# 192 unused bytes per partition in front of the first MLP layer's split input

## The chip, the core and the metric

The kernel runs on one core of one Trainium2 chip. The metric is the device time of one execution in microseconds (us); the times shown are of repeated executions of the same kernel.

## What is computed

A transformer block with modulated layer norms, for 8 batches of 1024 rows of 256 features, all in 32-bit floats. Per batch (cut to what matters):

```python
h = layernorm(x) * (1 + ca) + sa
attn = softmax((h * w_lhs) @ (h * w_rhs).T) @ h        # 1024 x 1024 scores
x = x + ga * attn
h = layernorm(x) * (1 + cb) + sb
x = x + gb * (relu(h @ W1 + b1) @ W2 + b2)             # 256 -> 1024 -> 256
```

The factors `sa`, `ca`, `ga`, `sb`, `cb`, `gb` are made once from a small input. The change touches the first product of the last line, `h @ W1`, and nothing else.

## The kernel before

**Split operands.** To keep precision, each 32-bit operand of a large product is held as two rounded parts, hi and lo (type fp32r), and a product is the sum of three matmuls: hi by hi, hi by lo, lo by hi. So the first layer has `W1hi`, `W1lo` as stationary operand (the weights that TensorE loads, 128 columns of 4 bytes, 512 bytes in each partition, per matmul) and `h2hi`, `h2lo` as moving operand (512 columns, 2048 bytes in each partition). `h2hi` is written by ScalarE (L819) and `h2lo` by VectorE (L1153), from the turned layer norm in `featT`.

**Steps.** The work of a batch is cut into steps, and the order of the steps on every engine is written out by hand (L29 to L170): in the loop over batches 2 to 6 (L121, `STEPS`), TensorE's list mixes the attention of this batch with the MLP of the batch before. On TensorE `SC.n` is a tile of scores (L649 to L651, operands `Lhi`, `Llo`, `Rhi`, `Rlo`), `AV.n` a tile of the attention product (L762, L763, L766, moving operand `V`, stationary `Phi`, `Plo`), `F.n` a group of the first MLP layer (L660 to L662) and `G.n` one of the second (L582, L583, L588, moving operand `W2hi`, `W2lo`, stationary `hid_hi`, `hid_lo`). Before `F.n` TensorE waits until ScalarE has read the result bank (`col_read`), and at the first of a half for `h2lo`.

One first-layer group is six matmuls, each with its own load of weights:

```python
for kk in range(DK):                                                          # DK = 2
    nc.tensor.matmul(col[n % 2][:], W1hi[:, kk, tile], h2hi[:, kk, cols], ...)   # L660
    nc.tensor.matmul(col[n % 2][:], W1hi[:, kk, tile], h2lo[:, kk, cols], ...)   # L661
    last = nc.tensor.matmul(col[n % 2][:], W1lo[:, kk, tile], h2hi[:, kk, cols], ...)   # L662
```

There are 16 groups a batch and 8 batches: 128 groups, 768 matmuls, 256 of each line. A second-layer group takes 12 matmuls of 256 columns, an attention tile 8 pairs (L762 with 258 columns, L763 with 256) and then 8 of L766 (258 columns).

**Where the operands lie.** Tensors are placed in each partition one behind the other, in the order in which L259 to L320 name them. With the sizes of that list the first bytes of those that matter are, and what is left of them when whole multiples of 512 are taken off:

| tensor | first byte | mod 512 |
|---|---|---|
| W1hi, W1lo | 17024, 25216 | 128 |
| W2hi, W2lo | 33408, 41600 | 128 |
| Phi, Plo | 87104, 99392 | 64 |
| Lhi, Llo, Rhi, Rlo | 111680 and on, 8192 apart | 64 |
| V | 144448, rows of 2080 bytes, second half 1040 behind | 64, and 32 more each row |
| hid_hi, hid_lo | 198336, 204480 | 192 |
| h2hi, h2lo | 210624, 218816 | 192 |

A tile of `W1` moves by 512 bytes, a half of `h2` by 2048 and `kk` by 4096, so all slices of one tensor have the same place mod 512. In what follows the **offset** is the place of the matmul's moving operand less the place of the weights that are loaded during it, those of the next matmul, mod 512. Within first-layer groups it is 192 - 128 = 64. In second-layer groups it is 128 - 192 = 448, in scores 0; in L766 it goes up by 32 from matmul to matmul: 16, 48, 80, 112, 144, 176, 208, and 240 for the eighth when `Phi`'s weights follow.

Other tensors lie behind `h2lo`: row statistics, maxima and other small ones (L310 to L320), up to byte 228,064.

Of the kernel before, what the change touches and what calls it, by code (L numbers as in the profile page):

```python
# [11 lines left out]
P = 128  # L12
# [200 lines left out]
def block_kernel(nc, x, w_lhs, w_rhs, W1, b1, W2, b2, cT, wmod, out):  # L213
# [39 lines left out]
    with ExitStack() as ctx:  # L253
        sb = lambda name, shape, dt=F32: ctx.enter_context(nc.sbuf_tensor(name, shape, dt))
# [51 lines left out]
        featT = sb("featT", [P, DK, HR])  # L306
        hid = sb("hid", [P, 2, HR])
        hid_hi, hid_lo = sb("hid_hi", [P, RING, HR], F32R), sb("hid_lo", [P, RING, HR], F32R)
        h2hi, h2lo = sb("h2hi", [P, DK, ROWS], F32R), sb("h2lo", [P, DK, ROWS], F32R)
        stats, stats1 = sb("stats", [P, HT, 6]), sb("stats1", [P, HT, 6])  # L310
        mv1, nm1, rs1 = sb("mv1", [P, T, 2]), sb("nm1", [P, T]), sb("rs1", [P, T])
# [1017 lines left out]
```

## Time and profile before

| | |
|---|---|
| median of 3 runs | 678.64 us (678.5 to 679.3) |
| the profiled execution's own time | 679.18 us |
| its span, first to last instruction | 677.4 us, 13532 instructions |
| TensorE busy, matmuls / weight loads | 672.5 us (99%) / 620.4 us (92%) |
| VectorE, ScalarE, GpSimd busy | 545.9 (81%), 500.2 (74%), 295.2 us (44%) |
| granted TensorE clock | 1.00 of full |

How to read it: a matmul's duration in the rows runs from its first column to its modelled end, and neighbours overlap. What a matmul costs in a stream is the distance from its start to the next one's start, called its spacing below; the timeline gives starts to 0.01 us, so spacings are taken over several matmuls. In the timeline, neighbours of one line are merged into one row (x8), which has the start of the first; a later window shows the row from a later one on.

### The profile page before, as it was taken

The numbers are of one execution on the slowest core, as the hardware profiler recorded it, in microseconds if no ns is written. First come the engines' busy times: TensorE is split into PE (matmuls) and PEld (weight loads), VectorE is DVE, ScalarE is ACT, GpSimd is POOL, SyncE is SP. The second block draws the span as 40 slices with busy tenths as digits, with TensorE's granted clock in tenths as the row PEclk, the third lists the DMA queues.
The fourth block names the chain that finished last, engine by engine and source line by source line (L and its number), as shares of the span: only waits on it lengthen the run. The fifth ranks groups of instructions, "written<-read, shape, count | busy, mean of one in ns | idle before, by whom it ended". The sixth has DMA issues, their size and how long they took to land.

```text
span 677.4 us, 13532 instructions
## 1 busy us (share of the span) xinstructions
PE 672.5 (99%) x4551; PEld 620.4 (92%) x4551; DVE 545.9 (81%) x1139; ACT 500.2 (74%) x749; POOL 295.2 (44%) x311
## 2 busy tenths in 40 slices
PE   9999999999999999999999999999999999999998
PEld 8688889998999999999999989999899999999897
DVE  4798889887899879998799887988789987778321
ACT  2376787976889777895878949888688976747563
POOL 3551365225353345442645235542535334615544
PEclk9999999999999999999999999999999999999999
DMA  8131664237632377124671256513763246311210
GB/s 295 55 81 62 194 188 148 72 97 237 194 96 74 123 238 231 48 89 149 202 210 62 93 186 195 145 62 124 216 195 84 75 146 197 97 41 65 85 48 31
DMA packets 72897, 88.57 MB, mean 131 GB/s; under 512 B 6880, under 2 KB 64800, under 8 KB 72864
## 3 DMA queue, kind: packets, MB, share of 16 engines
q1 hardware_dynamic: 72864, 88.15, 41.6%
q8 instruction: 18, 0.29, 0.2%
q14 instruction: 15, 0.12, 0.1%
HBM read 51.66 MB, written 36.47 MB: 130 GB/s over the span
## 4 chain that ended last, share of the span: by engine, by line
PE 99%; DVE 0%; DMA 0%; issue 0%; SPq 0%
PE col L662 9%; PE col L661 9%; PE col L660 9%; PE acc L582 8%; PE acc L583 8%; PE acc L588 8%; PE score L766 8%; PE score L762 8%; PE score L763 8%; PE score L650 4%; PE score L651 4%; PE score L649 4%; PE score L755 4%; PE score L623 2%; PE score L551 1%; PE score L727 1%
## 5 line engine op out<-in xcount | busy, mean ns | idle before, releaser
L1249 POOL TENSOR_TENSOR hid_lo<-hid,hid_hi 128x512 fp32r<-128x512 f32 x127 | 175.9, 1387 | 258.3 <-ACT hid_hi L791 257.6
L787 ACT ACTIVATE hid<-col,b1T 128x512 f32<-128x512 f32 x128 | 87.1, 681 | 72.6 <-PE col L662 67.8
L582 PE MATMUL acc<-W2hi,hid_hi 128*128 128x256 f32 x480 | 118.0, 280 | 0.0
L583 PE MATMUL acc<-W2lo,hid_hi 128*128 128x256 f32 x480 | 116.6, 277 | 0.0
L762 PE MATMUL score<-V,Phi 128*128 128x258 f32 x448 | 108.7, 281 | 0.0
L763 PE MATMUL score<-V,Phi 128*128 128x256 f32 x448 | 108.5, 281 | 0.0
L662 PE MATMUL col<-h2hi,W1lo 128*128 128x512 f32 x256 | 101.0, 395 | 0.0
L660 PE MATMUL col<-h2hi,W1hi 128*128 128x512 f32 x256 | 100.7, 393 | 0.0
L661 PE MATMUL col<-h2lo,W1hi 128*128 128x512 f32 x256 | 100.7, 393 | 0.0
L791 ACT ACTIVATE hid_hi<-hid 128x512 fp32r<-128x512 f32 x128 | 81.0, 633 | 23.2 <-PE acc L588 15.6
L582 PEld LDWEIGHTS acc<-W2hi,hid_hi 128*128 128x128 f32 x480 | 90.3, 188 | 1.4
L583 PEld LDWEIGHTS acc<-W2lo,hid_hi 128*128 128x128 f32 x480 | 90.2, 188 | 1.5
L762 PEld LDWEIGHTS score<-V,Phi 128*128 128x128 f32 x448 | 85.0, 190 | 0.7
L763 PEld LDWEIGHTS score<-V,Phi 128*128 128x128 f32 x448 | 84.1, 188 | 0.7
L588 PE MATMUL acc<-W2hi,hid_lo 128*128 128x256 f32 x480 | 76.4, 276 | 0.0
L876 ACT ACTIVATE soft<-soft 128x1024 f32<-128x1024 f32 x56 | 58.3, 1051 | 22.4 <-DVE soft L1027 11.8
L1064 DVE TENSOR_TENSOR Plo<-soft,Phi 128x1024 fp32r<-128x1024 f32 x56 | 70.9, 1283 | 2.1 <-ACT Phi L892 2.1
L588 PEld LDWEIGHTS acc<-W2hi,hid_lo 128*128 128x128 f32 x480 | 64.4, 188 | 0.0
L766 PE MATMUL score<-V,Plo 128*128 128x258 f32 x448 | 62.8, 282 | 0.0
L892 ACT ACTIVATE Phi<-soft 128x1024 fp32r<-128x1024 f32 x56 | 58.9, 1052 | 0.6
L1236 POOL TENSOR_SCALAR nm<-mv 128x4 f32<-128x4 f32 x32 | 11.6, 362 | 108.6 <-DVE mv L1085 64.9
L662 PEld LDWEIGHTS col<-h2hi,W1lo 128*128 128x128 f32 x256 | 48.2, 188 | 10.6
(168 smaller groups left out, 1476.5 us busy)
## 6 DMA issues: line engine op xcount, KB each, us to landing
block_rows<-blocks SPq DMA_DIRECT2D x29, 512.0 KB, 2.8
blocks<-block_rows SPq DMA_DIRECT2D x116, 128.0 KB, 2.9
x_cur<-x SPq DMA_DIRECT2D x16, 512.0 KB, 3.9
ln_t<-x SPq DMA_DIRECT2D x14, 512.0 KB, 4.8
score_blocks<-stage SPq DMA_DIRECT2D x14, 512.0 KB, 2.9
S<-score_blocks SPq DMA_DIRECT2D x56, 128.0 KB, 3.0
S<-quarter_blocks SPq DMA_DIRECT2D x56, 96.0 KB, 2.6
out<-x_mlp SPq DMA_DIRECT2D x8, 512.0 KB, 5.3
```

What stands on the lines that cost most here:

```text
L582: nc.tensor.matmul(o, hi, W2hi[:, it, :], start=(it == 0 and (apart or t % 2 == 0)), stop=False, skip_group_check=True)
L583: nc.tensor.matmul(o, hi, W2lo[:, it, :], start=False, stop=False, skip_group_check=True)
L588: last = nc.tensor.matmul(o, lo, W2hi[:, it, :], start=False, stop=(it == FT - 1), skip_group_check=True)
L660: nc.tensor.matmul(col[n % 2][:], W1hi[:, kk, tile], h2hi[:, kk, cols], start=(kk == 0), stop=False)
L661: nc.tensor.matmul(col[n % 2][:], W1hi[:, kk, tile], h2lo[:, kk, cols], start=False, stop=False)
L662: last = nc.tensor.matmul(col[n % 2][:], W1lo[:, kk, tile], h2hi[:, kk, cols], start=False, stop=(kk == DK - 1))
L762: nc.tensor.matmul(o, Phi[:, slot, t, :], V[:, t, 0:VW], start=(t == 0), stop=False)
L763: nc.tensor.matmul(o[:, 0:D], Phi[:, slot, t, :], V[:, t, VP:VP + D], start=False, stop=False)
L766: last = nc.tensor.matmul(o, Plo[:, slot, t, :], V[:, t, VP:VP + VW], start=False, stop=(t == T - 1))
L787: nc.scalar.activation(hid[:, n % 2, :], col[n % 2][:], ACT.Relu, bias=b1T[:, n % FT:n % FT + 1]).then_inc(col_read, 1)
L791: nc.scalar.activation(hid_hi[:, n % RING, :], hid[:, n % 2, :], ACT.Copy).then_inc(hid_hi_done, 1)
L1249: G.tensor_tensor(hid_lo[:, n % RING, :], hid[:, n % 2, :], hid_hi[:, n % RING, :].bitcast(F32), ALU.subtract).then_inc(hid_lo_done, 1)
```

## The change

A tensor of 48 floats, 192 bytes in each partition, is placed between `hid_lo` and `h2hi`. Nothing reads or writes it. All that lies behind it, `h2hi`, `h2lo` and the small tensors, moves up by 192 bytes.

```diff
         hid_hi, hid_lo = sb("hid_hi", [P, RING, HR], F32R), sb("hid_lo", [P, RING, HR], F32R)
+        sb("before_h2", [P, 48])
         h2hi, h2lo = sb("h2hi", [P, DK, ROWS], F32R), sb("h2lo", [P, DK, ROWS], F32R)
         stats, stats1 = sb("stats", [P, HT, 6]), sb("stats1", [P, HT, 6])
```

`h2hi` then begins at byte 210,816, which is 384 mod 512, and the offset within first-layer groups is 384 - 128 = 256.

## Rows read from the trace of the kernel before

**Rows 1.** The page: busy time by engine, and the granted clock in 40 slices.

```profile
span 677.4 us, 13532 instructions
...
PE 672.5 (99%) x4551; PEld 620.4 (92%) x4551; DVE 545.9 (81%) x1139; ACT 500.2 (74%) x749; POOL 295.2 (44%) x311
...
PEclk9999999999999999999999999999999999999999
```

**Rows 2.** The chain that ended last: shares of the 677.4 us span by line.

```profile
by line: PE col L662 8.8%; PE col L661 8.7%; PE col L660 8.7%; PE acc L582 8.2%; PE acc L583 8.1%; PE acc L588 8.0%; PE score L766 7.9%; PE score L762 7.8%; PE score L763 7.8%; PE score L650 4.4%; PE score L651 4.3%; PE score L649 4.3%; PE 
```

**Rows 3.** Groups by line (busy us, mean ns of one | idle before).

```profile
L662 PE MATMUL col<-h2hi,W1lo 128*128 128x512 f32 x256 | 101.0, 395 | 0.0
L660 PE MATMUL col<-h2hi,W1hi 128*128 128x512 f32 x256 | 100.7, 393 | 0.0
```

**Rows 4.** TensorE's timeline (start us, us, what), first-layer stretch behind the second layer.

```profile
182.44 0.39 PE L660 MATMUL col<-h2hi,W1hi 128*128 128x512 f32 x1
182.66 0.39 PE L661 MATMUL col<-h2lo,W1hi 128*128 128x512 f32 x1
182.89 0.39 PE L662 MATMUL col<-h2hi,W1lo 128*128 128x512 f32 x1
183.13 0.39 PE L660 MATMUL col<-h2hi,W1hi 128*128 128x512 f32 x1
...
185.19 0.28 PE L762 MATMUL score<-V,Phi 128*128 128x258 f32 x1
```

**Rows 5.** The same timeline, first-layer stretch behind the attention product.

```profile
188.04 0.40 PE L660 MATMUL col<-h2hi,W1hi 128*128 128x512 f32 x1
...
188.75 0.40 PE L660 MATMUL col<-h2hi,W1hi 128*128 128x512 f32 x1
...
192.24 0.28 PE L582 MATMUL acc<-W2hi,hid_hi 128*128 128x256 f32 x1
...
192.72 0.28 PE L582 MATMUL acc<-W2hi,hid_hi 128*128 128x256 f32 x1
```

**Rows 6.** Windows (busy us of each engine, PEclk the granted clock) over both stretches.

```profile
182.44:185.19 2.75, 2.75 (x14) 2.26 (x13) 2.72 (x4) 1.15 (x2) 0.00 (x0) 1.00 0.81 230
188.04:192.24 4.20, 4.20 (x20) 3.41 (x19) 4.08 (x8) 3.62 (x5) 2.51 (x3) 1.00 1.03 264
```

**Rows 7.** Timeline of TensorE, a settled second-layer group, 256 columns each.

```profile
172.43 0.28 PE L582 MATMUL acc<-W2hi,hid_hi 128*128 128x256 f32 x1
...
173.79 0.39 PE L660 MATMUL col<-h2hi,W1hi 128*128 128x512 f32 x1
```

**Rows 8.** Timeline of TensorE, score matmuls of 256 columns, no offset between operands.

```profile
155.17 0.28 PE L650 MATMUL score<-Rlo,Lhi 128*128 128x256 f32 x1
...
155.77 0.40 PE L649 MATMUL score<-Rhi,Lhi 128*128 128x512 f32 x1
```

**Rows 9.** Timeline of TensorE, one run of eight L766, read from its start and later ones.

```profile
626.04 1.12 PE L766 MATMUL score<-V,Plo 128*128 128x258 f32 x8
...
626.52 0.53 PE L766 MATMUL score<-V,Plo 128*128 128x258 f32 x3
...
626.65 0.40 PE L766 MATMUL score<-V,Plo 128*128 128x258 f32 x2
...
626.89 0.28 PE L766 MATMUL score<-V,Plo 128*128 128x258 f32 x1
627.00 0.28 PE L762 MATMUL score<-V,Phi 128*128 128x258 f32 x1
```

**Rows 10.** Groups by line: who writes the split input, and who follows a first-layer group.

```profile
L787 ACT ACTIVATE hid<-col,b1T 128x512 f32<-128x512 f32 x128 | 87.1, 681 | 72.6 <-PE col L662 67.8 <-POOL hid_lo L1249 4.3
...
L1153 DVE TENSOR_TENSOR h2lo<-featT,h2hi 128x512 fp32r<-128x512 f32 x32 | 21.6, 712 | 10.6 <-ACT h2hi L819 10.6
...
L819 ACT ACTIVATE h2hi<-featT 128x512 fp32r<-128x512 f32 x32 | 20.2, 633 | 1.0
```

## The prediction

> **What bounds the kernel.** The page is read first: TensorE is busy for 672.5 of 677.4 us, VectorE for 81%, and the granted clock is full, the 2.4 GHz level, in all 40 slices [rows 1]. The chain that ended last is TensorE nearly throughout; the three first-layer lines hold 8.8 + 8.7 + 8.7 = 26.2% of it [rows 2], 177.5 us of the span. Over 768 matmuls that is 231.1 ns each. They had no idle time before them [rows 3]. So no wait can be taken away here, and what the change can alter is how fast one matmul follows the next.
>
> The timeline shows that this is not one number. In a stretch behind the second layer, 12 first-layer matmuls take from 182.44 to 185.19, 2.75 us, 229 ns each [rows 4]. In a stretch behind the attention product, 18 of the same matmuls take from 188.04 to 192.24, 4.20 us, 233.3 ns each [rows 5]. Same line, shape, clock and addresses mod 512, and the matmuls busy throughout [rows 6]. In the first the starts 182.44, .66, .89 and 183.13 show steps of 0.22, 0.23, 0.24: the delay isn't even over the three lines.
>
> What would it be with no delay? The nearest row is a settled second-layer group: 12 matmuls of 256 columns from 172.43 to 173.79, 113.3 ns each, with weight loads back to back as well [rows 7]. Twice that for 512 columns is 226.7 ns, my estimate of the floor. Against it score matmuls of the same 256 columns with offset 0 take five in 0.60 us (155.17 to 155.77), 120.0 ns each, 6.7 over the floor [rows 8]; and the first-layer stretch at 233.3 is 6.6 over its floor, the same amount. A lost slot of some 6.7 ns a matmul is what I read from this, lost in one state of the stream and not in another.
>
> That place matters and not just shape is shown by the run of eight L766. All are 258 columns from V by 128 columns of Plo, only the offset goes up by 32 each time. The first four take 0.48 us (626.04 to 626.52); the fifth, at offset 144, 0.13 (to 626.65); the sixth and seventh together 0.24; the eighth, at offset 240 with Phi's weights behind it, 0.11 (626.89 to 627.00) [rows 9]. 0.11 is the floor for 258 columns (113.3 x 258 / 256 = 114 ns), 0.13 some 15 ns over it.
>
> **The change part by part.** (1) It adds no instruction, wait or transfer, and takes none away. (2) It moves h2hi and h2lo by 192 bytes, so the offset of the first-layer matmuls goes from 64 to 256. No row has 256 columns or more at offset 256; the nearest is offset 240, at the floor [rows 9]. Bounds: at best all 768 go to 226.7, 768 x (231.1 - 226.7) = 3.4 us less; at worst they all take 233.3, the worst stretch of this line that I found, 768 x 2.2 = 1.7 us more. Between them I take a value nearer to the row at 240, since that is 16 bytes away where offset 64 is 192 away, but not the floor itself, since one short matmul at a seam isn't a stream of 512 columns: the middle between the floor, 226.7, and the good stretch of now, 229.2, which is 228.0. That gives 768 x (231.1 - 228.0) = 2.4 us less.
>
> (3) The seams. Where a second-layer group follows a first-layer one, the second layer starts badly: four matmuls from 192.24 to 192.72 take 0.48 us, 120 ns each, instead of 113.3 [rows 5, 7], 27 ns in all. By the written order there are 37 such seams, 1.0 us. A first layer in another state may remove these or leave them; zero in the sum, 1.0 us in the lower end. (4) h2hi and h2lo are written by ScalarE and VectorE, 32 times each at 633 and 712 ns [rows 10], 42.9 us of busy time in all, on engines that are not the bound, and a start that is a multiple of 64 bytes before and after gives no row of theirs a reason to change. If one did by 5%, it would be 0.04 us a step, and what is late next is the first F of a half; VectorE has 19% idle to take it. (5) The small tensors behind move too; they are operands of 64 transposes and of short statistics. Zero. (6) A faster first layer asks ScalarE sooner: it needs 681 ns a group for L787 and as much again for the split, against some 1370 ns that six matmuls take. It had idle time before L787, 67.8 us of it waiting on TensorE [rows 10], so it follows.
>
> The sum: the profiled execution, 679.18 us, goes to 676.8. The median of the runs is 0.54 below the profiled one, so the forecast is 678.64 - 2.4 = **676.2 us**.
>
> **The rivals.** *No effect.* Two ways lead there. In the first, offset 256 is a place like any other, and the stream finds good and bad states there as it does at 64; the mean stays near 231. For it speaks that 229 and 233.3 both occur at one and the same offset [rows 4, 5], so the offset isn't all. It gives 678.6, within 1 us. In the second, the reads of the two operands don't touch each other at all and the different spacings come from something else; it gives 678.6 exactly. Against that stands the run of eight, with nothing changed but the place [rows 9]. The Trainium skill has this as a rule ("TensorE: Matmul & The Clock Gate", in "Step-by-step: what each phase is for"): the moving operand and the weights have two independent read ports, and loading the next weights doesn't take bandwidth from the running matmul. By it the padding would do nothing; the trace so far bears it out badly, as the spacings of rows 9 differ in 0.13 and 0.11, so I give this second way 8 in 100 of itself. That the padding does not move h2hi would come to the same; the tensors are placed one behind the other, so 2 in 100.
>
> *Slower.* The moving operand is read faster than the weights: 2048 bytes in about 230 ns, 8.9 bytes a ns, against 512 bytes in at most 113 ns [rows 7], 4.5 a ns. Read upward from their first byte, the moving operand gains 4.4 bytes a ns on the weights. If the two hinder each other where they come to the same place mod 512, the moving operand at offset 64 has 448 bytes to make up, 102 ns, just at the end of the load; at 256 it has 256, 58 ns, in the middle of it. Then each of the 768 has its meeting for certain, which may cost the 6.7 ns of rows 8: all at 233.3, 1.7 us more, **680.3**. For it speaks that offset 0, met at the outset, does lose this in its stream. Against it: at 448 they would meet 64 bytes in, after 15 ns, and the second layer is at the floor with that [rows 7]. It decides from a mean spacing above 233 ns on; the 15 ns over the floor at offset 144 would be worse still, but that was one matmul in eight and not a stream.
>
> **How the numbers follow.** A measurement of this kernel can tell about 0.2%, 1.4 us, from no change; that is 1.8 ns on each of the 768. Forecast, a mean under 229.3: 0.45. No effect: 0.20 for a like mix of states, 0.08 for independent reads, 0.02 for a padding that isn't there, 0.30 together. Slower, a mean of 232.9 and over: 0.25. The forecast's own range goes from the floor with the seams, 678.6 - 3.4 - 1.0 = 674.2, to 677.3; the other cases reach up to 680.3, and 0.1 is for the spread of runs. So 674.2 to 680.4 holds them but for something beyond the bounds, with at most 2 in 10 left out.
>
> **What would show it.** In the profile after, the stretch of 18 behind the attention product should shrink from 4.20 us to about 4.10 (228 ns each; 4.08 at the floor), and the 12 behind the second layer from 2.75 to about 2.73. The shares of the three first-layer lines should go from 26.2% to below 26%. If the slower case holds, both stretches stand at 233 or more. Second layer away from seams, scores and L766 should keep their 113.3, 120.0 and 0.13 / 0.11. What would make the prediction wrong: the same 2.75 and 4.20 (no effect), another order of states in which scores or the attention product after a first-layer group lose what that gains, or a new wait on ScalarE before L660, of which there is none now [rows 3].

## The result and the profile after

The changed kernel takes 681.57 us (median of 6 runs, 680.66 to 681.87) against 678.70 (678.50 to 679.79): a ratio of 1.0034, 95% interval 1.0025 to 1.0044, that is 1.7 to 3.0 us more. It got slower, and the part that was meant to get faster did so. Line numbers of this kernel are one higher than before from L309 on. Disturbed executions are left out of every number below: two of four of p224 (834.68 and 2392.38 us) and one of six of p448 (2392.39 us).

The page of the changed kernel, its span, busy times and granted clock:

```profile
span 678.9 us, 13532 instructions
...
PE 674.1 (99%) x4551; PEld 623.4 (92%) x4551; DVE 547.0 (81%) x1139; ACT 500.3 (74%) x749; POOL 295.4 (44%) x311
...
PEclk9999999999999999999999999999999999999999
```

The same instructions at the same clock, 1.6 us more of busy matmuls. Its chain that ended last, the shares by line, and one long piece of it (start us, us):

```profile
by line: PE col L661 8.7%; PE col L662 8.6%; PE col L663 8.6%; PE acc L583 8.3%; PE acc L584 8.2%; PE acc L589 8.2%; PE score L763 7.9%; PE score L767 7.9%; PE score L764 7.8%; PE score L651 4.3%; PE score L652 4.3%; PE score L650 4.3%; PE 
...
44.74 20.88 PE score L756 x96
```

The same piece in the kernel before:

```profile
45.39 20.88 PE score L755 x96
```

The first-layer lines (now L661 to L663) hold 8.7 + 8.6 + 8.6 = 25.9% of the chain where they held 26.2% [rows 2]; the second-layer lines (L583, L584, L589) hold 8.3 + 8.2 + 8.2 = 24.7%, where they held 8.2 + 8.1 + 8.0 = 24.3%. The second layer's operands did not move. The piece at 44.74 stood at 45.39 before, so this execution happens to have lost 0.65 us less ahead of it. The profiled executions differ by 1.48 us (680.66 against 679.18), with the 0.65 by 2.1; the medians differ by 2.87, and the profiled execution is the fastest of the six of the changed kernel.

The same stretches as in rows 4 and 5, in TensorE's timeline (start us, us, what), and the second-layer stretch behind the second of them:

```profile
182.20 0.40 PE L661 MATMUL col<-h2hi,W1hi 128*128 128x512 f32 x1
...
184.94 0.28 PE L763 MATMUL score<-V,Phi 128*128 128x258 f32 x1
...
187.81 0.40 PE L661 MATMUL col<-h2hi,W1hi 128*128 128x512 f32 x1
...
188.51 0.39 PE L661 MATMUL col<-h2hi,W1hi 128*128 128x512 f32 x1
188.74 0.39 PE L662 MATMUL col<-h2lo,W1hi 128*128 128x512 f32 x1
...
191.91 0.28 PE L583 MATMUL acc<-W2hi,hid_hi 128*128 128x256 f32 x1
...
192.38 0.28 PE L583 MATMUL acc<-W2hi,hid_hi 128*128 128x256 f32 x1
...
194.74 0.28 PE L763 MATMUL score<-V,Phi 128*128 128x258 f32 x1
```

Behind the second layer 12 first-layer matmuls take 182.20 to 184.94, 2.74 us (2.75 in rows 4). Behind the attention product 18 take 187.81 to 191.91, 4.10 us (4.20 in rows 5), 228 ns each; the last 15 of them, from 188.51 on, take 3.40 us, 226.7 ns each, the floor of the prediction. Then the second layer: four matmuls to 192.38, and 20 more to 194.74, 2.36 us, **118 ns each**. The same 20 ended at the following row in the kernel before, 2.26 us behind 192.72 [rows 5], 113 ns each:

```profile
194.98 0.28 PE L762 MATMUL score<-V,Phi 128*128 128x258 f32 x1
```

The windows of the two stretches (TensorE and weight loads busy throughout the second, the clock full):

```profile
187.81:191.91 4.10, 4.10 (x20) 3.38 (x19) 3.98 (x8) 3.55 (x5) 2.41 (x3) 1.00 1.01 255
192.38:194.74 2.36, 2.36 (x22) 2.36 (x21) 2.21 (x5) 2.30 (x4) 1.00 (x1) 1.00 0.00 0
```

In the second, the slow one, there is no DMA traffic at all (last two columns 0.00 and 0), so it isn't traffic that slows it.

**Where the time went.** The starts of all 4551 matmuls are in the trace, so the spacing can be summed by kind. The floor is the prediction's, 113.3 ns for 256 columns [rows 7] and in proportion for other widths. Over it, before and after, waits left out: first layer 3.3 and 1.7 us, second layer 1.6 and 4.6, attention product 6.5 and 7.0, scores 2.4 and 2.4. In means: first layer 231.0 to 228.9 ns, 768 x 2.1 = 1.6 us won; second layer 114.4 to 116.4, 3.1 us lost over 1512 matmuls; attention product 0.5 lost. Together 2.1 us more by the traces, within the interval of the runs (1.7 to 3.0).

**When the second layer is slow.** The timeline of the changed kernel shows both kinds within 4 us:

```profile
205.13 0.28 PE L583 MATMUL acc<-W2hi,hid_hi 128*128 128x256 f32 x1
...
205.60 0.28 PE L583 MATMUL acc<-W2hi,hid_hi 128*128 128x256 f32 x1
...
206.51 0.40 PE L661 MATMUL col<-h2hi,W1hi 128*128 128x512 f32 x1
...
207.90 0.28 PE L583 MATMUL acc<-W2hi,hid_hi 128*128 128x256 f32 x1
...
209.31 0.28 PE L763 MATMUL score<-V,Phi 128*128 128x258 f32 x1
```

A second-layer group behind an attention tile: 12 matmuls from 205.13 to 206.51, 1.38 us, and its last eight, from 205.60, in 0.91, 114 ns each. The next such group stands behind a first-layer group: 12 matmuls from 207.90 to 209.31, 1.41 us, no part of it faster. Over the whole trace, going by the last four matmuls of each stretch, 29 of 29 second-layer stretches behind attention end fast (near 113 ns) in both kernels; behind the first layer 37 of 37 do before and 2 of 37 after. So in the changed kernel the second layer starts in a slow pace there and stays in it, up to 36 matmuls on end. These 37 stretches hold 2.0 of the 3.1 us. Nearly all of the rest, 1.1 us, stands in 6 stretches of 24 or 48 matmuls that come behind a first-layer stretch too, but with the four transposes of `MB` in between; of the 12 stretches behind `MB` the other 6, which have attention or the second layer ahead of it, end fast.

### The profile page after: what moved, and what is told of

It reads as the page before. It is cut to its first block, busy times and chain, and to the rows that moved or that the text cites. A ratio compares the mean times of both kernels' runs of the same rounds, so it can differ in the third digit from the quotient of the medians.

```text
span 678.9 us, 13532 instructions
## 1 busy us (share of the span) xinstructions
PE 674.1 (99%) x4551; PEld 623.4 (92%) x4551; DVE 547.0 (81%) x1139; ACT 500.3 (74%) x749; POOL 295.4 (44%) x311
## 4 chain that ended last, share of the span: by engine, by line
PE 99%; DVE 0%; DMA 0%; issue 0%; SPq 0%
PE col L661 9%; PE col L662 9%; PE col L663 9%; PE acc L583 8%; PE acc L584 8%; PE acc L589 8%; PE score L763 8%; PE score L767 8%; PE score L764 8%; PE score L651 4%; PE score L652 4%; PE score L650 4%; PE score L756 4%; PE score L624 2%; PE score L552 1%; PE score L728 1%
## 5 line engine op out<-in xcount | busy, mean ns | idle before, releaser
L583 PE MATMUL acc<-W2hi,hid_hi 128*128 128x256 f32 x480 | 119.3, 282 | 0.0
L584 PE MATMUL acc<-W2lo,hid_hi 128*128 128x256 f32 x480 | 117.9, 279 | 0.0
L661 PE MATMUL col<-h2hi,W1hi 128*128 128x512 f32 x256 | 100.4, 392 | 0.0
L663 PE MATMUL col<-h2hi,W1lo 128*128 128x512 f32 x256 | 99.8, 390 | 0.0
L583 PEld LDWEIGHTS acc<-W2hi,hid_hi 128*128 128x128 f32 x480 | 90.6, 189 | 1.4
L584 PEld LDWEIGHTS acc<-W2lo,hid_hi 128*128 128x128 f32 x480 | 90.5, 189 | 1.3
L589 PE MATMUL acc<-W2hi,hid_lo 128*128 128x256 f32 x480 | 77.7, 279 | 0.0
L589 PEld LDWEIGHTS acc<-W2hi,hid_lo 128*128 128x128 f32 x480 | 65.3, 188 | 0.0
L663 PEld LDWEIGHTS col<-h2hi,W1lo 128*128 128x128 f32 x256 | 48.1, 188 | 10.5
```

Of the source, the lines that this page charges most:

```text
L583: nc.tensor.matmul(o, hi, W2hi[:, it, :], start=(it == 0 and (apart or t % 2 == 0)), stop=False, skip_group_check=True)
L584: nc.tensor.matmul(o, hi, W2lo[:, it, :], start=False, stop=False, skip_group_check=True)
L589: last = nc.tensor.matmul(o, lo, W2hi[:, it, :], start=False, stop=(it == FT - 1), skip_group_check=True)
```

## The experiments

All offsets are given as in the text ahead of the prediction. Where a tensor is put in front of another, it stands on that line, so that line numbers are those of before. The means are those of all first- and second-layer matmuls, without those that come 30 ns or more over the floor (waits); in split the cut matmuls are left out of the first layer's mean. Each ratio is to the kernel before as it ran beside that kernel (medians of 678.7 to 679.0 us).

| kernel | bytes in front of | first layer | seam to second | second layer | first, ns | second, ns | median, us | ratio to before (95%) |
|---|---|---|---|---|---|---|---|---|
| before | - | 64 | 0 | 448 | 231.0 | 114.4 | 678.70 | |
| changed | h2: 192 | 256 | 192 | 448 | 228.9 | 116.4 | 681.57 | 1.0025 to 1.0044 |
| p512 | h2: 512 | 64 | 0 | 448 | 231.0 | 114.4 | 678.82 | 0.9990 to 1.0008 |
| all192 | W1: 192 | 64 | 0 | 448 | 231.0 | 114.4 | 679.02 | 0.9993 to 1.0012 |
| w2_192 | W2: 192 | 256 | 0 | 448 | 229.4 | 116.4 | 680.81 | 1.0018 to 1.0038 |
| p256 | h2: 256 | 320 | 256 | 448 | 231.0 | 114.4 | 679.49 | 0.9995 to 1.0013 |
| p448 | h2: 448 | 0 | 448 | 448 | 228.9 | 116.4 | 681.43 | 1.0021 to 1.0047 |
| p64 | h2: 64 | 128 | 64 | 448 | 231.8 | 115.4 | 681.45 | 1.0027 to 1.0055 |
| p128 | h2: 128 | 192 | 128 | 448 | 232.8 | 114.1 | 680.21 | 1.0009 to 1.0028 |
| p32 | h2: 32 | 96 | 32 | 448 | 234.2 | 114.6 | 681.74 | 1.0025 to 1.0059 |
| p160 | h2: 160 | 224 | 160 | 448 | 233.2 | 116.2 | 683.43 | 1.0050 to 1.0083 |
| p224 | h2: 224 | 288 | 224 | 448 | 233.3 | 115.0 | 682.49 and 681.81 | |
| g256_f256 | hid: 192 | 256 | 0 | 256 | 229.1 | 119.6 | 686.26 | 1.0091 to 1.0125 |
| g384_f256 | hid: 64, h2: 128 | 256 | 128 | 384 | 229.2 | 119.4 | 686.09 | 1.0092 to 1.0126 |
| g320_f256 | hid: 128, h2: 64 | 256 | 64 | 320 | 228.7 | 117.6 | 682.41 | 1.0033 to 1.0064 |
| split | h2: 192 | 256 | 128 | 448 | 229.2 | 116.4 | 684.55 | 1.0062 to 1.0096 |
| order_p0 | - | 64 | 0 | 448 | 230.4 | 114.4 | 685.18 | 1.0077 to 1.0104 |
| order_p192 | h2: 192 | 256 | 192 | 448 | 229.2 | 115.9 | 687.28 | 1.0105 to 1.0136 |

### Do only offsets count, and in what unit?

```diff
-        h2hi, h2lo = ...
+        sb("before_h2", [P, 128]); h2hi, h2lo = ...      # p512; [P, 64] in p256, [P, 112] in p448
```

```diff
-        W1hi, W1lo = ...
+        sb("before_W1", [P, 48]); W1hi, W1lo = ...       # all192
```

p512:

> 512 bytes instead of 192 in front of h2hi, so that only the place moves and the offset mod 512 stays 64 as before. Theory A (the spacing of first-layer matmuls, and the state that the second layer inherits from them, go by places mod 512): the same as before, 678.7 us within 0.7, first-layer stretch behind the attention product 4.20 us for 18, settled second layer 113.3 ns. Rival (any move of h2 or of the small tensors behind it costs something, or the place counts in another unit): 680 us or more, as after the change.

all192:

> The 192 bytes stand in front of W1hi, so that weights, attention operands, hidden layer and h2 all move by 192 and every offset between two operands of TensorE stays as before. Theory A with offsets between operands only: the same as before, 678.7 us within 0.7. Rival (the absolute place mod 512 of a moving operand counts, here 384 for h2 as after the change): about 681 us, second layer at 117 to 118 ns behind a first-layer stretch.

Both are the kernel before over again, in the time (0.9999 and 1.0003 of it) and in both means. So neither the added tensor, nor the move of the small tensors behind it, nor the absolute place of an operand costs anything; what counts is where TensorE's operands lie relative to each other.

p256:

> 256 bytes instead of 192 in front of h2hi: offset 320 in the first layer, 256 at the seam to the second. Theory A says that the time can differ from both; if the slow second layer comes from a first layer at its floor (rival C), a first layer that is at 229 ns or more leaves it at 113.3 and the total near 678.7, and one at 226.7 leaves it at 117.7 and the total near 681. If neither 226.7 nor 229 and over is found with such a second layer, C falls.

TensorE's timeline of p256, the stretch behind attention:

```profile
187.39 0.40 PE L660 MATMUL col<-h2hi,W1hi 128*128 128x512 f32 x1
...
191.59 0.28 PE L582 MATMUL acc<-W2hi,hid_hi 128*128 128x256 f32 x1
```

4.20 us as before, and every mean is that of before to 0.1 ns, at offset 320 instead of 64. The places differ by 256. So the unit looked like 256, not the 512 of the change's own reckoning. One pair can agree by chance; p448 tests another, at the changed kernel's place.

p448:

> 448 bytes in front of h2hi, 256 more than the change: first layer at offset 512, that is 0, seam at 448. Mod 512 this is a new place, mod 256 it is the changed kernel's in every offset. If the unit is 256 bytes: the changed kernel over again, 681.5 us within 0.7, first-layer stretch of 18 in 4.10 us, second layer 118 ns behind it. If p256 was like before by chance only: anything, and a first layer at the scores' offset 0 with 231 ns is then the likeliest.

It is the changed kernel over again: 681.43 against 681.57 us, 228.9 and 116.4 ns, and the same counts of slow stretches (35 of 37 behind the first layer, none of 29 behind attention). Two pairs agree in everything, and places 128 bytes apart differ (64 from 192, 0 from 128 in the table), so the unit is 256 bytes and not 128.

### What leaves the second layer slow?

w2_192 puts the 192 bytes in front of W2hi, so that only the seams change:

```diff
-        W2hi, W2lo = ...
+        sb("before_W2", [P, 48]); W2hi, W2lo = ...
```

> The 192 bytes stand in front of W2hi: the first layer has offset 256 as after the change, second layer 448, scores 0 and attention product as ever, but at the seam from first to second layer h2 (384) and hid_hi (384) are at offset 0 as before the change, where after it they are at 192. Theory B (the seam's offset decides in which state the second layer starts): first layer near 226.7 ns, second layer back at 113.3 ns, time 677 us or less. Rival C (the first layer's own fast state of 226.7 ns leaves the second layer in its slow state of 117.7 ns, whatever the seam): about 681 us as after the change, second layer at 117.7 behind it.

TensorE's timeline of w2_192, the stretch behind attention and the second layer behind it:

```profile
187.77 0.40 PE L660 MATMUL col<-h2hi,W1hi 128*128 128x512 f32 x1
...
191.92 0.28 PE L582 MATMUL acc<-W2hi,hid_hi 128*128 128x256 f32 x1
...
192.39 0.28 PE L582 MATMUL acc<-W2hi,hid_hi 128*128 128x256 f32 x1
...
194.74 0.28 PE L762 MATMUL score<-V,Phi 128*128 128x258 f32 x1
```

The seam is at offset 0 as it was before, and the second layer still takes 2.35 us for the 20 matmuls from 192.39 to 194.74; all 37 stretches behind the first layer end slow. Theory B, the seam's own offset, falls. Theory C holds here. The 18 of the first layer take 4.15 us here against 4.10, though their own offset is the same: they take longer to reach the floor behind attention, which has other offsets at the seam (229.4 ns in the mean against 228.9).

p64 and p128 try two more places of the first layer:

> 64 bytes in front of h2hi: first layer at offset 128. Offsets 64 and 320 gave one and the same kernel to 0.01 us, so the unit is 256 bytes or less. If it is 128, offset 128 is the same place as 256: first layer at 228.9 ns mean, second at 116.4, about 681 us. If it is 256, this is a third place that no run has shown: the first layer's mean lies somewhere from 226.7 to 235 ns, and by theory C (a first layer at its floor leaves the second layer at 117.7 ns, one above it leaves it at 113.3) the second layer is slow only where the first is at 226.7.

> 128 bytes in front of h2hi: first layer at offset 192. Unit 128: the same as before the change, 678.7 us, first layer 231.0, second 114.3. Unit 256: the fourth place, the one that the second layer has with itself (448 less 256), where it settles at its floor. Then the first layer should settle at 226.7 ns too, and if theory C holds in the form that any first layer at its floor leaves the second slow, about 681 us; if the second layer takes over a state that fits its own place, it is at 113.3 throughout and the time is 675 to 676 us.

Neither is any earlier kernel, as the unit of 256 wants, and p128 comes out at neither of the times named for it. p128 gives the first layer the offset at which the second runs at its floor, and it is not at its floor there. Its stretch of 18 behind attention, in the timeline:

```profile
188.15 0.40 PE L660 MATMUL col<-h2hi,W1hi 128*128 128x512 f32 x1
...
192.35 0.28 PE L582 MATMUL acc<-W2hi,hid_hi 128*128 128x256 f32 x1
```

4.20 us; what a place is worth depends on the shape of the matmul too. All 37 second-layer stretches behind it end fast. p64 is the case that C does not stand: its first layer is at 231.8 ns, well over its floor, and still 24 of 37 stretches behind it end slow. It isn't the predecessor's speed that is handed on: 20 first-layer stretches of p64 stand behind the second layer and all end at 230 ns; what follows the 13 short ones (6 matmuls) ends fast, what follows the 7 long ones (12 matmuls) ends slow.

split cuts the last first-layer matmul ahead of each seam of the changed kernel:

```diff
-    last = nc.tensor.matmul(col[n % 2][:], W1lo[:, kk, tile], h2hi[:, kk, cols], ...)
+    for cs in [slice(0, HR)] if kk == 0 or not seam else [slice(0, HR - 16), slice(HR - 16, HR)]:
+        last = nc.tensor.matmul(col[n % 2][:, cs], W1lo[:, kk, tile], h2hi[:, kk, ...], ...)
```

> The changed kernel with the last first-layer matmul ahead of each of the 37 seams to the second layer cut in two, 496 and 16 columns, so that addresses and offsets stay and only the moment at which the second layer starts moves. Each cut adds one matmul that waits for its own weight load, about 107 to 113 ns, 4 us in all. Theory E (the second layer inherits a state of timing from the matmuls ahead of it, and keeps it): the second layer's mean falls from 116.4 to about 114.3 ns, 3.1 us back, 682 us in all. Rival (the addresses alone decide, now that h2 is at its new place): the second layer stays at 116.4 ns and the time is about 685.5 us.

The page of split has 4588 matmuls and as many loads, 37 more of each. The median rose by 3.0 us over the changed kernel, the sums over the floor, waits and all, by 3.8 (I had put down 4), and the second layer stayed at 116.4 ns, with 36 of 37 stretches slow. Most of the cost is a pause: the second layer's first matmul has 200 ns to its next at each of the 37 seams, 3.2 us over the floor in all. The slow pace outlasts it. So theory E falls in this form: moving the moment of the seam, by the one amount tried, doesn't set the second layer free. The cut also moves the seam's offset from 192 to 128, which the expectation overlooked; but p128 has 128 there and all of its 37 stretches end fast, so that place by itself doesn't keep them slow.

### Is it the step ahead, or the changed kernel as a whole?

order_p0 and order_p192 change TensorE's written order in the middle loop (`STEPS`, which begins at L99), on the kernel before and on the changed one:

```diff
-        ... SC.4 F.2- F.3- G.0- F.4- G.1- SC.5 SC.6 F.5- SC.7 G.2- G.3- F.6- F.7-
-        MB.0 G.4- G.5- G.6- G.7- F.8- F.9- AV.0 F.10- F.11- F.12- G.8- G.9- AV.1 AV.2 MB.1 G.10- AV.3 G.11-
-        F.13- G.12- AV.4 ...
+        ... SC.4 G.0- F.2- F.3- F.4- SC.5 G.1- G.2- SC.6 F.5- SC.7 G.3- G.4- F.6- F.7-
+        MB.0 G.5- G.6- G.7- F.8- F.9- AV.0 G.8- G.9- F.10- F.11- F.12- AV.1 AV.2 MB.1 G.10- AV.3 G.11-
+        G.12- F.13- AV.4 ...
```

> The changed kernel with TensorE's written order in the middle loop altered so that the second-layer groups 0, 1, 4, 8, 9 and 12 stand behind a score tile, an attention tile or another such group and no longer behind a first-layer group; 5 to 7 still follow one. Theory F (a second-layer stretch keeps the state that its predecessor left: slow behind a first-layer stretch of the changed kernel, fast behind attention or scores): six groups of 12 matmuls in 5 batches fall by some 4 ns each, 1.4 us in all, and the time from 681.5 to about 680. Rival G (with h2 at its new place the second layer is slow wherever it stands in the pipeline): 681.5 or more. New waits of TensorE, if the order brings any, come on top in both and show as spacings over 30 ns above the floor.

> The same order on the kernel before, as the control: its second-layer groups settle at 113.3 ns behind all kinds of steps, after a poor first half of a group behind a first-layer one. Theory F: within 0.6 us of 678.8, and so order_p192 gains some 1.4 us more from the order than this. Rival G: both move by the same.

The order itself is a bad one. The waits of TensorE in order_p192 (who waited for whom: us, times, longest):

```profile
PE acc L582 <- ACT hid_hi L791: 3.4, 5, 0.7
...
PE acc L588 <- POOL hid_lo L1249: 0.9, 5, 0.2
```

Five batches wait for `hid_hi`, whose writer could no longer keep ahead, and the waits in the second layer grow from 1.1 us to 8.0 in both kernels. So both of the times expected, about 680 and 679, are missed, by 7 and 6 us, and the medians don't tell the theories apart: 687.28 - 685.18 = 2.1 us where changed and before differ by 2.9, but the first layer's gain shrank as well in this order, from 1.6 to 0.9 us. What tells is the second layer's sum over the floor, waits left out: it fell from 4.6 to 3.8 us in the changed kernel and from 1.55 to 1.52 in the control. So a different predecessor cures some of it, in the changed kernel alone: theory F in direction, with 0.8 us instead of 1.4.

The stretches behind scores account for the rest: 6 of 17 of them end slow, and none of 17 in order_p0. The trace tells which. All 6 have a score tile of six matmuls ahead of them and 12 or 18 first-layer matmuls ahead of that; with 6 first-layer matmuls ahead of the same score tile, 10 of 10 end fast. So the slow pace is handed through a score tile, and whether there is one goes with how long the first layer ran, as in p64. Directly behind an attention tile no second-layer stretch with offset 448 ends slow in any kernel (29 of 29 fast in each; of 34 in the order kernels the 5 others end in one of the waits, in both alike). One step further it isn't so clean: in p224 two of the five stretches that have an attention tile and then `MB` ahead of them end slow.

### Is there a place for hid_hi that goes with the first layer's new one?

```diff
-        hid_hi, hid_lo = ...
+        sb("before_hid_hi", [P, 48]); hid_hi, hid_lo = ...     # g256_f256; [P, 16] in g384_f256, [P, 32] in g320_f256
```

> The 192 bytes stand in front of hid_hi: first layer at offset 256 as after the change, second layer at 256 too instead of 448. By the unit of 256 the second layer then has the place that scores have, where five matmuls of 256 columns took 120.0 ns each. Theory D (what a 256-column stream settles at goes by its own offset): second layer near 120 ns, 1512 matmuls by 3.6 ns more than the 116.4 after the change, about 686 us. Theory C' (after a first layer at its floor a second layer of the same offset goes on at its floor): 113.3 ns and 676 us.

> 64 bytes in front of hid_hi and 128 in front of h2hi: first layer at offset 256 as after the change, second layer at 384 (128 by the unit of 256). Theory C says that the state in which the first layer leaves the stream is a slow one for the second layer's offset 448; at another offset it need not be. Second layer at 113.3: 676 us; at 117.7: 681; at 120: 686. The first layer's own floor of 226.7 behind the attention product should stay in any case, since its offset does.

> 128 bytes in front of hid_hi and 64 in front of h2hi: first layer at offset 256 as after the change, second layer at 320 (64 by the unit of 256), the one multiple of 64 not yet tried for it. At 256 and 384 the second layer stood at 119.4 to 119.6 ns in the mean. If 192 (448) is the only place at which it can settle at its floor, 119.5 ns and about 686 us; if the slow state after the first layer is a matter of these two offsets together, it may be at 113.3 and 676 us.

The timeline of g256_f256 over the same 20 second-layer matmuls:

```profile
194.09 0.28 PE L582 MATMUL acc<-W2hi,hid_hi 128*128 128x256 f32 x1
...
196.49 0.28 PE L762 MATMUL score<-V,Phi 128*128 128x258 f32 x1
```

2.40 us, 120.0 ns each, as the scores of the same shape and offset [rows 8]: theory D holds for this place. At 384 it is 119.4 in the mean and at 320 it is 117.6, and there even the stretches directly behind attention all end slow (29 of 29). But at 320 the floor can be reached: the five stretches behind attention and `MB` run at it, such as this one of 12 matmuls:

```profile
202.35 0.28 PE L583 MATMUL acc<-W2lo,hid_hi 128*128 128x256 f32 x1
...
203.60 0.28 PE L762 MATMUL score<-V,Phi 128*128 128x258 f32 x1
```

Its last 11 matmuls take 1.25 us, 114 ns each. So at two of the four multiples of 64, 192 (448) and 64 (320), the second layer has a fast and a slow pace, and only at 448 did most stretches find the fast one; at 256 and 384 none of the 85 ended under 117 ns. No combination beat the kernel before.

### Places between the multiples of 64

> 160 bytes in front of h2hi, first layer at offset 224, half way between 192 (mean 232.8 ns, second layer 114.1) and 256 (228.9 and 116.4). If only whole blocks of 64 bytes count, it equals one of these two. If each 16 or 32 bytes counts, it is a place of its own; the second layer's mean, between 114.1 and 118, then decides over the total, at 0.76 us for each 0.5 ns, against 0.38 us for each 0.5 ns of the first layer's mean.

> 224 bytes in front of h2hi, first layer at offset 288, half way between 256 (228.9 and 116.4 ns) and 320 (231.0 and 114.3). Blocks of 64 alone: one of these two, 681.4 or 678.8 us. A place of its own otherwise; the sum of both excesses decides.

> 32 bytes in front of h2hi, first layer at offset 96, half way between 64 (231.0 and 114.3 ns) and 128 (231.8 and 115.4). By the unit of 256 bytes it stands apart from all that ran. Blocks of 64 alone: one of those two, 678.8 or 681.4 us.

Each is a place of its own: the first layer is at 233.2, 233.3 and 234.2 ns, worse than at either neighbour. So blocks of 64 alone are not the rule either; in all three a start that is a multiple of 32 and not of 64 was worse for the first layer than any multiple of 64.

## Why the prediction was wrong

**What bounds the kernel** was right: TensorE's spacing alone moved, and no wait came or went. The 18 behind attention came out at 4.10 us, the figure given, the 12 behind the second layer at 2.74 (2.73 given), and the three lines' share below 26%.

**The step that failed is (3), the seams**, with what stands under "what would show it", that the second layer away from seams keeps 113.3 ns. I had seen that the second layer starts badly behind the first (27 ns in four matmuls), took that for a cost of the seam that ends with it, and put it at zero, or 1.0 us of gain. In the changed kernel the start is no worse, but the stream does not recover: 117.7 to 118 ns to the end of the stretch, 3.1 us in all, twice what the first layer won. The sum had no term for it and the range no bound on that side; 681.57 us lies above its 680.4. The last of the signs of being wrong came near, "another order of states", but named the scores and the attention product, which lost 0.1 and 0.5 us, and gave it neither price nor chance. Rows 4 and 5 had shown the thing already, one and the same first-layer stream at 229 ns for 12 matmuls or 233 for 18 on end, by what ran ahead of it; I read it as a state of the first layer and did not ask which of its neighbours would inherit a new one.

**Step (2), the first layer**, was right in sign and mis-sized: 231.0 to 228.9 ns, 1.6 us, where I had 228.0 and 2.4. It was right for a bad reason. The sign was luck: I went by the nearest row, offset 240, at its floor; but the mean is 232.8 at 192, 233.2 at 224, 228.9 at 256 and 233.3 at 288, so 16 or 32 bytes of nearness say nothing. It also went by mod 512, where the unit is 256, so offset 256 was not a new place: the scores stand at it [rows 8]. Steady, their 256 columns lose 6.7 ns there and the first layer's 512 lose none, so that row would have misled too.

**Steps (1), (4), (5), (6)** hold: p512 moves the same tensors and costs nothing, and no wait came. (The 42.9 us in (4) are 43.0 by count and mean, and 41.8 by the busy times of rows 10; nothing hangs on it.)

**The rivals.** *No effect* fell in both ways: the first layer's mean left 231 for 228.9 ns, and the time rose. Only an unread tensor was added, 1.6 us went from one layer and 3.1 us to another, and p512 and all192 show that nothing but places relative to each other does it. The Trainium skill says that moving operand and weights have two independent read ports, and that a load takes nothing from the running matmul ("TensorE: Matmul & The Clock Gate", "Step-by-step: what each phase is for"). By that the padding does nothing; for these back-to-back fp32r streams, with a weight load of 128 columns for each matmul, the spacings show otherwise, and the measurement decides. That it is the two reads that hinder each other is the nearest reading of this, not shown. *Slower* had the sign and, at 680.3, a figure within 1.3 us, by the wrong mechanism: the first layer did not go to 233 ns. Its picture of two readings that meet at one place is not borne out: by it 256 and 320 would both be worse than 64 for the first layer, and 256 ran fastest and 320 as 64. Its rate for the weights wasn't measured either: 113 ns is the spacing of the loads, and a load's own row lasts 188 ns (L660 in the trace of before).

What stays open is the mechanism inside TensorE. The runs show a unit of 256 bytes, spacings that repeat to 1 ns, and states that a stream keeps and hands on; they don't show what it is that is out of step, nor whether a matmul's own weights or the next ones' count, since inside a stretch both lie at the same place. Neither a model of it nor a rule to foretell the state of an untried place came out.

## What to carry to other kernels

In a kernel bound by back-to-back fp32r matmuls, the bytes between tensors can be worth about 1% (678.7 to 686.3 us here), so they are to be measured over a handful of paddings. Judge such a change by the spacing of every kind of matmul and not of the one whose operand moved: the stream hands its state on, and the loss stood in a layer whose addresses had not changed. And here it was the offset of the moving operand to the weights mod 256 bytes that counted; of two paddings that differ by 256 one run was enough.

## What the runs showed of the hardware

- Spacing repeats mod 256 bytes of offset: 64 and 320 gave 231.0 / 114.4 ns, 256 and 0 gave 228.9 / 116.4; a shift of everything together changes nothing (all192).
- A stream of 256-column matmuls has two steady spacings, 113.3 and 117.7 ns, at offset 448 and at 320; at offset 0 (scores, rows 8) and 256 (g256_f256) it has 120.0. A 512-column stream at 256 settles at 226.7, at 64 at 229 or 233.3.
- In units of 16 cycles at the 2.4 GHz level (6.67 ns) these means are 17, 17 2/3, 18, 34, 34 1/3 and 35, worked out from the spacings. A single matmul does not lose a whole unit, though: in the slow pace of the changed kernel the spacings are 117 to 119 ns one by one, and at 229 they go round as 226, 229 and 232.
- 17 units, 113.3 ns for 256 columns, is 6% over 106.7 ns, which is 256 cycles of that level, and no second-layer stretch of any run had a mean below those 113.3.
- A slow pace outlasts other work: in the changed kernel four transposes (`MB`) between first and second layer let it through in 6 of 6 cases, and in split a pause of 200 ns at the seam in 36 of 37.
